# Cross-attention and FFN on one core: head weights loaded in the value stage, output product first in late steps, seven blocks in the down stage

## The reference

```python
x = x + xattn(layernorm(x), ctx, ctx, mask, Wq, Wk, Wv, Wo)   # 32 query heads, 8 kv heads of 128
x = x + ffn(layernorm(x), w1, w2, w3)                         # hidden 1376

# xattn: q, k get rotary phases; logits = 30*tanh(q.k*0.0884/30), masked, softmax; attn @ Wo
# ffn:   w1, w2, w3 are first rounded to NF4 (per 64 elements: absmax, 16-value code), and
#        y = (silu(x @ w1.T) * (x @ w2.T)) @ w3.T
```

## Time and profile before

| | |
|---|---|
| time, 3 runs | 856.96 us median (856.88 to 857.13) |
| profiled execution | 855.72 us, span of its instructions 853.9 us |
| PE | 803.7 us busy, 94% |
| VectorE | 684.7 us, 80% |
| ScalarE | 465.5 us, 55% |
| GpSimd | 497.8 us, 58% |
| granted PE clock, mean | 0.982 |
| DMA | 91.76 MB, 107 GB/s |

### The profile page before, as it was taken

The page is one execution under the profiler, slowest core; times in us unless marked ns, Lnnn a source line. Parts: engine busy times, 40 slices in busy tenths (PEclk is TensorE's granted clock), DMA queues, the critical chain, the costliest instruction groups (busy, mean ns, idle before and its releaser), DMA issues.

```text
span 853.9 us, 10691 instructions
## 1 busy us (share of the span) xinstructions
PE 803.7 (94%) x3806; PEld 644.9 (76%) x3806; DVE 684.7 (80%) x745; ACT 465.5 (55%) x571; POOL 497.8 (58%) x270
## 2 busy tenths in 40 slices
PE   6798997999999999999999999998879999995998
PEld 4677885777788778877787778776668788884886
DVE  3876862589989899989989889889858999999512
ACT  5014752665665765665666656656325686866410
POOL 2545154776985986978977978967200344544100
PEclk9999998999999999999999999999999999997999
DMA  9676646432343433442533533412301121302112
GB/s 330 192 196 185 188 102 188 133 99 75 109 132 75 125 116 87 124 120 71 167 87 77 157 83 96 132 38 72 108 0 50 50 93 50 117 26 59 55 35 99
DMA packets 63541, 91.76 MB, mean 107 GB/s; under 512 B 6784, under 2 KB 30464, under 8 KB 63488
## 3 DMA queue, kind: packets, MB, share of 16 engines
q1 hardware_dynamic: 62304, 88.25, 35.7%
q10 hardware_dynamic: 1184, 2.82, 0.9%
HBM read 51.00 MB, written 19.07 MB: 82 GB/s over the span
## 4 chain that ended last, share of the span: by engine, by line
PE 81%; DVE 11%; issue 3%; DMA 2%; POOL 1%; ACT 1%; SPq 1%; DVEq 0%; POOLq 0%
PE bank L508 7%; PE bank L510 7%; PE bank L509 7%; PE bank L524 7%; PE bank L526 6%; PE bank L525 6%; PE avp L598 6%; PE bank L570 6%; PE bank L490 5%; PE bank L492 5%; PE bank L491 5%; PE trp L497 4%; DVE nfv L927 2%; PE bank L699 2%; PE bank L700 2%
## 5 line engine op out<-in xcount | busy, mean ns | idle before, releaser
L1247 POOL TENSOR_TENSOR eb<-eb,maskf 128x512 f32<-128x512 f32 x64 | 100.8, 1575 | 60.6 <-ACT eb L801 60.6
L799 ACT ACTIVATE eb<-bank 128x512 f32<-128x512 f32 x64 | 38.2, 597 | 177.6 <-PE bank L570 177.6
L1190 POOL TENSOR_TENSOR qT<-cs_loop,sw 128x512 f32<-128x512 f32 x57 | 101.9, 1787 | 34.8 <-DMA sw<-cs_loop 34.5
L508 PE MATMUL bank<-xh,wqh 128*128 128x512 f32 x256 | 106.5, 416 | 1.2 <-POOL wql L1181 1.2
L524 PE MATMUL bank<-woh,ath 128*128 128x512 f32 x256 | 107.6, 420 | 0.0
L526 PE MATMUL bank<-woh,atl 128*128 128x512 f32 x256 | 101.5, 396 | 0.0
L510 PE MATMUL bank<-xh,wql 128*128 128x512 f32 x256 | 101.5, 396 | 0.0
L525 PE MATMUL bank<-wol,ath 128*128 128x512 f32 x256 | 101.2, 395 | 0.0
L509 PE MATMUL bank<-xl,wqh 128*128 128x512 f32 x256 | 101.2, 395 | 0.0
L927 DVE SCALAR_TENSOR_TENSOR nfv<-nfq,nfv 128x1408 f32<-128x1408 uint8 x42 | 85.5, 2037 | 0.7
L935 DVE TENSOR_TENSOR cs_loop<-bank,csq 128x1024 f32<-128x1024 f32 x57 | 69.1, 1213 | 18.8 <-PE bank L510 18.8
(11 more groups left out here) (150 smaller groups left out, 1983.7 us busy)
## 6 DMA issues: line engine op xcount, KB each, us to landing
sw<-cs_loop SPq DMA_DIRECT2D x114, 128.0 KB, 2.3
stage<-wq_pieces SPq DMA_DIRECT2D x32, 256.0 KB, 3.0
stage<-wo_pieces SPq DMA_DIRECT2D x32, 256.0 KB, 2.8
stage<-dq_scratch SPq DMA_DIRECT2D x32, 256.0 KB, 3.6
sw<-cs_start SPq DMA_DIRECT2D x46, 128.0 KB, 2.3
ks_scratch<-qT SPq DMA_DIRECT2D x16, 256.0 KB, 2.5
vs_scratch<-vst SPq DMA_DIRECT2D x16, 256.0 KB, 3.2
kcur<-ks_scratch SPq DMA_DIRECT2D x16, 256.0 KB, 2.9
```

The costliest lines, as they stand in the source:

```text
L508: nc.tensor.matmul(o, wqh[:, g, k, :], xh[:, k, cs], start=k == 0, stop=False)
L1190: nc.gpsimd.tensor_tensor(dst, products(ru, slot)[:, 0, :], sw[:, slot, :], ALU.add).then_inc(roped, 1)
```

## The change

Four places, in the order in which they run:

- The four first pieces of head 1's weights are loaded in steps 14 and 15 of the value stage; the store of NF4 chunk 0 goes behind the key and value loads. GpSimd makes the low parts of pieces 30 and 31 one rope earlier. ScalarE does `weights(1)` before `high(32)`.
- NF4 positions: 122 by slot 60 (before 116), 43 over the first 20 FFN slots and none in the last two (before 50 over 22), 11 in the down rounds 1 to 6 (before 10 in rounds 0 to 4); the signs of the down stage no longer run a round ahead of the additions.
- In head steps without a projection (57 to 63) PE does `out_unit(j - 1)`, then weight and token transposes, and only then the transposes of `nrm`. The second layer norm is cut up: moments of blocks 0 and 1 in step 59, the rest in 60, blocks 2 and 3 over 61 and 62, 4 and 5 over 63 and the end.
- Down stage: block 6 joins the rounds in bank `lgp`, so all transposes but those of tile 1 use `trp`; the first high part `down_hi(0)` comes right after the last `silu`.

```diff
@@ nf_before
             if slot <= NSTEP:
-                return 2 * min(max(0, slot - 2), 58)
+                return 122 * min(max(0, slot - 2), 58) // 58
             if slot <= NSTEP + 2 * HT:
-                return 116 + 50 * (slot - NSTEP) // (2 * HT)
-            return min(166 + 2 * (slot - NSTEP - 2 * HT), 16 * 11)
+                return 122 + min(43 * (slot - NSTEP) // 20, 43)
+            return min(165 + 2 * (slot - NSTEP - 2 * HT), 16 * 11)
@@
+        def w3_bank(n):
+            return lgp if n == 1 else trp
@@ SP, value stage
+                if v >= 14:
+                    head_piece(2 * v - 28)
+                    head_piece(2 * v - 27)
                 c, b = v // B, v % B
                 wait(sp, v_copied, v + 1)
...
-            nf_store(0)
             for i in range(4):
                 wait(sp, v_out[i], 64)
...
             sp.dma_start(vcur[:, 4:8, 0:DH], vs_d[0, 1]).then_inc(v_in[1], 16)
-            for p in range(4):
-                head_piece(p)
+            nf_store(0)
@@ PE, head loop
+                    alone = j + AHEAD >= NUNIT
+                    if alone:
+                        out_unit(j - 1)
+                    if last and b in (3, 4):
+                        weight_transposes(b - 3)
+                    if last and b in (5, 7):
+                        token_transposes(b - 5)
+                        token_transposes(b - 4)
                     pe.wait_ge(an_done, j + 1)
                     wait(pe, at_lo, j)
                     transpose4(trp, lambda g: nrm[:, b % 2, g * 128:(g + 1) * 128]).then_inc(at_done, 1)
-                    if j > 0:
+                    if j > 0 and not alone:
                         out_unit(j - 1)
-                    if last and b in (3, 4):
-                        weight_transposes(b - 3)
-                    if last and b in (5, 6):
-                        token_transposes(2 * b - 10)
-                        token_transposes(2 * b - 9)
@@ PE, down stage
-                wait(pe, wt_lo, m - 1)
-                transpose4(trg[m % 2], lambda i: stage[:, m % 4, i * 128:i * 128 + p], p).then_inc(wt_done, 1)
+                wait(pe, wt_lo, m if n > 2 else m - 1)
+                transpose4(w3_bank(n), lambda i: stage[:, m % 4, i * 128:i * 128 + p], p).then_inc(wt_done, 1)
...
-                for b in range(6):
+                for b in range(7):
+                    if n == 0 and b == 6:
+                        pe.wait_ge(wt_lo, 2 * HT + 2)
                     last = down(b, n, outs[b])
...
-            for b in range(6, B):
-                pe.wait_ge(final_done, b - 5)
-                for n in range(HT):
-                    last = down(b, n, outs[b - 6])
-                last.then_inc(down_done, 1)
+            pe.wait_ge(final_done, 1)
+            for n in range(HT):
+                last = down(B - 1, n, outs[0])
+            last.then_inc(down_done, 1)
@@ ACT
             weights(0)
+            weights(1)
             high(32)
-            weights(1)
...
                 silu(n)
+                if n == 2 * HT - 1:
+                    down_hi(0)
                 if n > 0:
                     hidden_hi(n - 1)
-                for c, i in nf_signs(NSTEP + n):
-                    nf_above_bound(c, i)
+                if n < 2 * HT - 1:
+                    for c, i in nf_signs(NSTEP + n):
+                        nf_above_bound(c, i)
             hidden_hi(2 * HT - 1)
...
+            for n in range(1, HT):
+                down_hi(n)
+                for c, i in nf_signs(NSTEP + 2 * HT + n - 2):
                     nf_above_bound(c, i)
@@ DVE, head loop
+                    if last and b in (4, 5):
+                        weight_lo(b - 4)
+                    if last and b == 4:
+                        dve.wait_ge(roped, NK + NUNIT)
+                        ln_rstd(1, range(0, 2))
+                        normalise(0, sw)
+                        normalise(1, sw)
+                    if last and b == 5:
+                        dve.wait_ge(y_done, NSTEP - 4)
+                        ln_moments(2, range(2, 4))
+                    if last and b == 6:
+                        token_lo(0, 1, xt_bank(0))
+                        token_lo(1, 1, xt_bank(1))
+                        ln_rstd(2, range(2, 4))
+                        normalise(2, sw)
+                        normalise(3, sw)
+                    if last and b == 7:
+                        dve.wait_ge(y_done, NSTEP - 2)
+                        ln_moments(3, range(4, 6))
+                        token_lo(2, 1, xt_bank(2))
+                        token_lo(3, 1, xt_bank(3))
                     dve.wait_ge(at_hi, j + 1)
                     nc.vector.tensor_tensor(atl[:, j % 4, :], trp[:, :], as_f32(ath[:, j % 4, :]),
                                             ALU.subtract).then_inc(at_lo, 1)
+                    if last and b == 3:
+                        dve.wait_ge(y_done, NSTEP - 6)
+                        ln_moments(1, range(0, 2))
...
-            add_out(NSTEP - 2)
-            dve.wait_ge(y_done, NSTEP - 1)
-            ln_stats(3, range(4, 6))
+            ln_rstd(3, range(4, 6))
             normalise(4, sw)
             normalise(5, sw)
+            add_out(NSTEP - 2)
@@ DVE, down stage
-                for c, i in nf_adds(NSTEP + 2 * HT + n):
+                for c, i in nf_adds(NSTEP + 2 * HT + n - 1) if n > 0 else ():
                     nf_add(c, i)
@@ POOL
-                if u in (1, 3):
-                    for n in (28 + u - 1, 29 + u - 1):
+                if u in (1, 2):
+                    for n in (26 + 2 * u, 27 + 2 * u):
                         weight_low(n)
...
-                    if last and b == 4:
+                    if last and b == 3:
                         power(1, range(0, 2))
```

More of the change, by code:

```diff
@@ L349, in k_store, with head_piece @@
                 sp.dma_start(ks_d[u % 8, u // 8], qT[:, u % 8 // 4, u % 4, :]).then_inc(k_out[u % 8], 16)
+            def head_piece(p):
+                kv, i = p // 8, p % 8
+                if kv < NKV - 1:
+                    src = wq_d[(kv + 1) * 4 + i] if i < 4 else wo_d[(kv + 1) * 4 + i - 4]
+                    piece(32 + p, src, p % 4)
             for n in range(5):
@@ L813, in head @@
                         weights(j + 2)
+                    if last and b in (3, 4):
+                        weight_hi(b - 3)
+                    if last and b in (5, 7):
+                        token_hi(b - 5)
+                        token_hi(b - 4)
                     act.wait_ge(at_done, j + 1)
@@ L818, in head @@
                         nf_above_bound(c, i)
[L819 to L826, removed]
             def weight_hi(n):
@@ L848, in hidden_hi, with down_hi @@
                 nc.scalar.activation(hh[:, t, half * 512:(half + 1) * 512], hf[:, n % 2, :], ACT.Copy).then_inc(h_hi, 1)
+            def down_hi(n):
+                m = 2 * HT + n
+                p = 128 if n < HT - 1 else HLAST
+                act.wait_ge(wt_done, m + 1)
+                if n == 0:
+                    act.wait_ge(gate_done, 2 * HT)
+                nc.scalar.activation(w3h[0:p, n, :].rearrange("h (a r q) -> h a q r", a=2, q=2),
+                                     w3_bank(n)[0:p, :].rearrange("h (a q r) -> h a q r", a=2, q=2), ACT.Copy)\
+                    .then_inc(wt_hi, 1)
             weights(0)
+            weights(1)
             high(32)
-            weights(1)
             for kv in range(NKV):
@@ L872, in _ @@
                 silu(n)
+                if n == 2 * HT - 1:
+                    down_hi(0)
                 if n > 0:
                     hidden_hi(n - 1)
-                for c, i in nf_signs(NSTEP + n):
-                    nf_above_bound(c, i)
+                if n < 2 * HT - 1:
+                    for c, i in nf_signs(NSTEP + n):
+                        nf_above_bound(c, i)
             hidden_hi(2 * HT - 1)
[L878 to L884, removed]
-                                     trg[m % 2][0:p, :].rearrange("h (a q r) -> h a q r", a=2, q=2), ACT.Copy)\
-                    .then_inc(wt_hi, 1)
-                for c, i in nf_signs(NSTEP + 2 * HT + n):
+            for n in range(1, HT):
+                down_hi(n)
+                for c, i in nf_signs(NSTEP + 2 * HT + n - 2):
                     nf_above_bound(c, i)
@@ L1085, in head @@
                                             ALU.subtract).then_inc(at_lo, 1)
-                    if last and b == 4:
-                        dve.wait_ge(y_done, NSTEP - 5)
-                        dve.wait_ge(roped, NK + NUNIT)
-                        ln_stats(1, range(0, 2))
-                        normalise(0, sw)
-                        normalise(1, sw)
-                    if last and b == 5:
-                        weight_lo(0)
-                        weight_lo(1)
-                        dve.wait_ge(y_done, NSTEP - 4)
-                        ln_moments(2, range(2, 4))
-                        for i in range(2):
```

(16 more changed lines are left out.)

6 lines of the change are left out of this document (2 added, 4 removed).

## The result

The changed kernel takes 838.59 us (median of 4 runs, 837.29 to 839.92), the kernel before 857.05 in the same job: ratio 0.9782, 95% interval 0.9764 to 0.9800, so 18.5 us faster. The prediction was 841 (835.5 to 848). The profiled execution took 837.29 with a span of 835.5, 18.4 under the span before.

What follows compares the result with a forecast made beforehand. PE works 804 of 853.9 us, so the time is its work plus its gaps. Terms -3.8 + 0 - 5.8 + 0.4 - 11.1 + 4.4 = -15.9 give a median of 841.1, said as 841; 80% range 835.5 to 848.

Steps and rivals of the forecast that it cites:

- A: End of value stage: earlier second-head weights let PE resume at 146.9, gated by GpSimd; -3.8 us (-8.1 to 0).
- B: Head loop: 5 more NF4 additions fit in VectorE's free time, cost 0 for PE.
- bound of +8: Head loop: cost if additions beside GpSimd work came on the path, half of 3.63 us in six three-addition steps.
- C: Steps 57 to 63: product before transposes, VectorE setting the pace in 57 to 59; -5.8 us (-10 to 0).
- Rival 3: Late steps gain nothing, the low half being late in each: 847 us; chance 0.11.
- The first FFN step: `nf_prepare(9)` and one addition, instead of two additions, ahead of the token low halves: +0.4 us (0 to 2.7).
- D: FFN end and down-stage start: 7 fewer additions, products 2.4 us after the FFN's last; -11.1 us (-12.5 to -3).
- rival 2: VectorE still lags at the end of the FFN, `hf` 3.4 us late as before: 846 us; chance 0.11.
- E: Down stage: last NF4 chunk's addition moves to round 6, so PE waits on its load; +4.4 us.
- Rivals 1 and 5: Last NF4 chunk not late, 836.6 us, chance 0.14; early loads reach ScalarE no earlier, 845 us, chance 0.05.
- Rival 4: Down loop: VectorE's and ScalarE's chain of sign and additions stalls the rounds, 863 us; chance 0.03.

Runs made afterwards that it cites:

- e8: Changed kernel with the 122 NF4 positions taken by slot 57, none in steps 57 to 59: 835.37 us.
- e9: Changed kernel with the NF4 positions of the kernel before (116 by slot 60, 50 over 22 FFN slots, then 2 a round): 843.44 us.
- e7: Changed kernel with `weight_low(32)` ahead of `nf_normalise(1)` in GpSimd's queue: 834.85 us.
- e5: Changed kernel with six token blocks in the down rounds, not seven, and blocks 6 and 7 behind them: 841.33 us.
- e2: Kernel before with only the late-step edits (output product first in steps 57 to 63, layer norm in pieces), old NF4 schedule: 848.13 us.
- e12: Kernel before with only the output product ahead of the `nrm` transposes on PE in steps 57 to 63: 853.55 us.
- e6: Changed kernel with the last NF4 chunk's additions three to a down round (rounds 1 to 4), not two: 836.35 us.
- e1: Kernel before with only the early loads of head 1's weights and the GpSimd and ScalarE order at the value stage's end: 852.88 us.
- e3: Kernel before with only the NF4 schedule and the down stage of the change: 851.83 us.
- e10: Changed kernel with the three edits of e6, e7 and e8 together: 829.43 us.
- e11: e10 with 120 NF4 positions by slot 58 and 45 over 21 FFN slots: 832.54 us.
- e4: Changed kernel unaltered, run again: 838.70 us.

## Why the prediction was right

**A**, right in the wait: GpSimd's chain from 141.84 gated PE at 147.01 (forecast 146.9). The half clock was charged with 1.6 and cost 1.5, partly by luck. The reason given, 1.1 us of work in the 5.6 before, is off: PE had 2.7 us of work in the 5.4 before 147.01, as projection and logits ran until 143.2. And what followed this same wait of 2.6 us differs: from the second to the third attention product it is 12.24 here, 10.70 in e8 at full clock, 13.23 in e9 with twelve slow matmuls. e7 shows the wait's part by taking it away.

**B**, right: no wait in the loop, and 425.7 us between steps 2 and 57 in both kernels. Two sizes in it were wrong. VectorE took on 17.1 us there, not 11, as the additions also became longer (1.96 us to 2.05 in the mean); its free time, 44 us before, hid that too. And the bound of +8 does not follow: half of 3.63 in six steps is 10.9. e8 shows how near the edge B was: twelve steps with three additions, not six, cost 3.7 us. The rule of the Trainium skill (page "SBUF — State Buffer", section "Who interferes with whom") that I weighed against B did not decide here, but it fits e8, where PE waits for masks of 1.91 us in the mean, 1.67 in the changed kernel. No run shows the port itself.

**C**, mechanism right, size 0.7 short. Product 59 was predicted 23.1 us after step 57's attention product and came 22.4 after it (581.22 to 603.59). Its waits were forecast as 2, 2 and 3.5 us; they were 1.3, 1.0 and 2.2. So the 0.7 was won ahead of product 59: its seven additions took 14.8 us, not 7 x 2.23 = 15.6. From there to the first FFN product it was 23.3 us, forecast 23.2 with the 0.8 for the clock. The half clock did strike product 59 and cost 1.0, as e5 shows, where it did not: VectorE's work hid the rest of its 1.6. Rival 3 is refuted by e2 and e12, which also show that the layer norm in pieces carries about half of C.

**The first FFN step**: +0.3 for +0.4.

**D**, right: the products start 2.17 us after the FFN's last (762.90 to 765.07), forecast 2.4, and at full clock. e9 shows that with the seven additions put back none of it is left; rival 2 did not occur (`hf` waited 3.12 us for ScalarE).

**E**, the term that was mis-sized most: +2.8, forecast +4.4. The place and the cause are right (e5 and e6). From the last addition's end to the landing it took 8.9 us (795.15 to 804.09), where I had taken 9.85 from before: the load landed in 3.0 us and not 3.7 to 4.0. And I charged half of the clock's 1.6, but the granted clock behind the wait was 1.00. That was luck: in e8 it fell behind 2.48 us at this place and cost 1.5, so a charge of half was fair. These two, 1.6 us, and C's 0.7 are most of the 2.5 us by which the span came out below the sum (-18.4 for -15.9).

**Rivals** 1 and 5 did not occur. Rival 4, the chain of the down loop: an addition took 1.6 to 1.7 in each round (3.36 for two), with GpSimd idle, so the chain of 4.6 stayed under the round of 5.23; even at 4.55 (e5) PE had no wait for `w3l`.

## What to carry to other kernels

When one engine is the bound and another is nearly full beside it, look for the places where the first waits for the second and count the second's work queued ahead of that very instruction; moving the optional part of it (here the NF4 additions) to where it has room was worth more here than reordering (D -11.3, the order alone -3.9). A gap closed shows the next engine in the chain, so read what is late next before the edit is made: here the order of three GpSimd instructions was worth as much as the loads that exposed it. Gains at separate gaps add up as long as the second engine's work moves along with the first's (e1 to e3 and e10 were forecast to within 1 us that way), but spare time on the second engine must be looked for in each stretch, not at its end (e11). What half clock costs behind a wait of 2 to 3 us is a chance and not a fixed price: over equal code it was 0 or 1.0 to 2.5 us.

## What the runs showed of the hardware

- Equal waits do not always bring the clock down. Behind 2.57 us at 147.01 it fell to 0.50, in e8 at the same place behind 2.57 it stayed at 1.00. Behind 2.24 us at product 59 it fell, in e5 at the same place it stayed. Behind 2.57 us at 804.09, after 36 us without a gap, it stayed, in e8 behind 2.48 after 36 us without a gap it fell. So a wait of 2.2 to 2.6 us is a risk of 1.0 to 1.5 us here (2.5 in e9), and what decides it is not shown. Behind 10 us it fell in every profile (before, e1, e2, e9, e12), for eight to twelve matmuls.
- The Trainium skill, page "TensorE: Matmul & The Clock Gate", section "What's actually happening", has idle against activity as the cause. Every fall in these rows follows a wait, which agrees; that equal waits differ is what these runs add.
- The changed kernel's runs lie within 2.6 us, and the profiles put a difference of that size into the key and value stages: the second attention product starts between 143.28 and 146.26 in kernels that are equal up to there (e4 to e6). The kernel before varies too (854.5 to 860.6 in later jobs). Some profiles have half-clock stretches in these stages, behind waits of PE for VectorE near 30, 45 or 71 us (e5 and e6 near 30 and 72), and the two of 143.28 and 143.71 have none. But e9 has two, near 45 and 72, and is at 143.34, so this is not the whole of the spread, which stays open.
- From the issue of the last chunk's store to HBM (0.7 MB, at 797.82) to the landing of the first piece loaded from it (256 KB, at 804.05) it took 6.2 us, the longest piece of the chunk's chain.
